# GpSimd's second addition for the dot products goes behind the stage's second gather; r follows it ahead of the third

## The reference

```
r = edge_vec / jnp.linalg.norm(edge_vec, axis=1, keepdims=True)
sh1 = SQRT3 * r
xs, xd = (x[edge_src], x[edge_dst])
v1 = jnp.concatenate([xs[:, 8:].reshape(E, 8, 3), xd[:, 8:].reshape(E, 8, 3)], axis=1)
vdot1 = jnp.einsum('euk,ek->eu', v1, sh1) / SQRT3
s_t = a1 * (jnp.einsum('eu,euw->ew', s1, Wss) + jnp.einsum('eu,euw->ew', vdot1, Wvv))
```

## Time and profile before

| | us |
|---|---|
| median of 3 runs | 6613.86 (6610.04 to 6614.21) |
| the profiled execution's own time | 6605.81 |
| its span | 6604.0 |
| PE busy | 5916.6 (90%) |
| DVE busy | 5987.5 (91%) |
| ACT busy | 4058.7 (61%) |
| POOL busy | 5021.9 (76%) |

### The profile page before, as it was taken

How to read it: one execution, slowest core, us unless ns; L and a number is a source line. 1 busy time by engine, 2 the same in 40 slices (tenths; PEclk the granted TensorE clock), 3 DMA queues, 4 the chain that set the end, 5 groups by cost and what they waited for, 6 DMA issues and landing times.

```text
span 6604.0 us, 217789 instructions
## 1 busy us (share of the span) xinstructions
PE 5916.6 (90%) x67802; PEld 5648.0 (86%) x67802; DVE 5987.5 (91%) x7727; ACT 4058.7 (61%) x12100; POOL 5021.9 (76%) x6871
## 2 busy tenths in 40 slices
PE   2999999999999999999999999999989999999997
PEld 2888888888888888888888888888888888888887
DVE  6999999999999999999999999999999999999998
ACT  3666666666666666666666666666666666666664
POOL 4777777777777777777777777777777777777774
PEclk9999999999999999999999999999999999999998
DMA  4444444444444444444444444444444444444442
GB/s 126 86 89 84 86 87 85 85 87 86 84 86 88 84 87 86 84 86 88 84 86 88 84 86 88 84 88 86 86 89 84 86 88 84 88 86 86 87 85 54
DMA packets 1671528, 569.93 MB, mean 86 GB/s; under 512 B 1535556, under 2 KB 1619493, under 8 KB 1670946
## 3 DMA queue, kind: packets, MB, share of 16 engines
q1 hardware_dynamic: 1568321, 516.43, 35.3%
q0 software_dynamic: 103168, 53.03, 6.0%
HBM read 302.19 MB, written 7.26 MB: 47 GB/s over the span
## 4 chain that ended last, share of the span: by engine, by line
PE 75%; issue 13%; DVE 5%; ACT 3%; another core or an unknown queue 3%; DVEq 1%; ACTq 0%; DMA 0%; POOL 0%; SPq 0%; POOLq 0%
PE p L982 42%; PE pw L977 18%; PE p L1068 4%; PE ph L965 2%; PE ph L954 2%; PE p L1061 2%; PE p L1063 1%; PE p L1029 1%; PE p L1011 1%; DVE prods L1275 1%; ACT hot_t L741 1%; PE p L1012 1%; DVEq L1434 1%; ACT osum L820 0%
## 5 line engine op out<-in xcount | busy, mean ns | idle before, releaser
L982 PE MATMUL p<-identity,prods 128*128 128x128 f32 x29016 | 3642.6, 279 | 7.8 <-issue 6.7
L647 POOL DMA_INDIRECT nodes<-x_rows,idx x3224 | 3114.5, 966 | 603.7 <-issue 515.9
L982 PEld LDWEIGHTS p<-identity,prods 128*128 128x128 f32 x29016 | 3292.0, 146 | 36.5 <-issue 12.3
L977 PE MATMUL pw<-w_stack,hid_t 128*128 128x128 bf16 x22568 | 1702.4, 223 | 116.2 <-issue 52.4
L977 PEld LDWEIGHTS pw<-w_stack,hid_t 128*128 128x128 bf16 x22568 | 1433.6, 100 | 216.7 <-issue 98.2
L1275 DVE TENSOR_TENSOR prods<-pw,M 128x1024 f32<-128x1024 f32 x806 | 977.1, 1212 | 38.5 <-PE pw L977 24.8
L1233 DVE TENSOR_TENSOR prods<-pw,V 128x2048 f32<-128x2048 f32 x403 | 914.4, 2269 | 9.4 <-ACT acc L926 6.3
L1252 DVE TENSOR_TENSOR prods<-pw,S 128x1024 f32<-128x1024 f32 x403 | 491.8, 1220 | 327.6 <-remote 190.7
L838 ACT ACTIVATE off_hot<-node_iota,off_base 128x42 f32<-128x42 f32 x3216 | 752.6, 317 | 13.0
L1285 DVE TENSOR_TENSOR prods<-pw,VT 128x1536 f32<-128x1536 f32 x403 | 705.2, 1750 | 23.9 <-PE pw L977 19.4
L594 POOL TENSOR_TENSOR msg<-th,late 128x128 f32<-128x128 f32 x403 | 164.0, 407 | 728.7 <-ACT th L819 390.8
(11 more groups left out here) (130 smaller groups left out, 8205.5 us busy)
## 6 DMA issues: line engine op xcount, KB each, us to landing
dstb<-in_dst SPq DMA_DIRECT2D x403, 504.0 KB
nodes<-x_rows,idx POOLq DMA_INDIRECT x3224
emb_stack<-emb_parts SPq DMA_DIRECT2D x2418, 20.0 KB
emb<-in_emb_t SPq DMA_DIRECT2D x403, 40.0 KB
hid_t<-hid_parts SPq DMA_TRANSPOSE x806
idx<-in_src SPq DMA_DIRECT2D x403, 4.0 KB
xw<-x SPq DMA_DIRECT2D x403, 7.9 KB
vecs<-in_vec SPq DMA_DIRECT2D x403, 12.0 KB
```

Source lines behind the costliest of these rows:

```text
L647: nc.gpsimd.indirect_dma_start(nodes[:, p, t, side, :], None, x_rows, bass.IndirectOffsetOnAxis(ap=idx[:, p, side, t:t + 1], axis=0)).then ...
L977: mm = nc.tensor.matmul(pw[:, slot, t, :], hid_t[:, layer, a.par, t, :], w2_stack[:, lo:lo + W], start=True, stop=True)
L982: return nc.tensor.matmul(out, column, identity[:, :], start=first, stop=last, is_transpose=True)
```

## The change

`along_rest` is cut in two. Its first addition (L614) stays between the first and the second gather. The second one, with its wait for `vr_two_done`, becomes `along_last` and is called behind the second gather, ahead of `directions`. So the program has r still between the second and the third gather, and the subtraction of the edge attributes alone between the third and the fourth.

```
             pool.wait_ge(vr_done, a.n(1, 1))
             nc.gpsimd.tensor_tensor(vr_two[:, :, :], vr[:, 0, :, :], vr[:, 1, :, :], ALU.add).then_inc(vr_two_done, 1)
+
+        def along_last(a):
+            p = a.par
             pool.wait_ge(vr_two_done, a.n(1, 1))
             nc.gpsimd.tensor_tensor(S[:, p, :, 2 * C:4 * C], vr_two[:, :, :], vr[:, 2, :, :], ALU.add
                                     ).then_inc(vdot_done, 1)
...
                     along_rest(two)
                 if zero is not None:
                     gathers(zero, 0, (1,))
+                if two is not None:
+                    along_last(two)
                 if one is not None and i != -1:
                     directions(one)
                 if zero is not None:
                     gathers(zero, 0, (2,))
```

## The result

The median of four runs went from 6614.03 us (6610.04 to 6622.14) to **6455.94 us** (6442.14 to 6466.6), a ratio of 0.9758 [0.9736, 0.9781]. The forecast was 6614 us with a range down to 6601, so 158 us were missed. The profiled execution of the changed kernel took 6466.6 us by its own time, 139 us less than that of before (6605.81).

A forecast was written before the change was run, and what follows sets the result against it. DVE (91%) and PE (90%) were taken to bound the kernel, POOL having slack ahead of L594. Terms summed to 0 in the turns and 0 at the start, so the 6613.86 us median gave 6614 us, range 6601 to 6628.

The forecast's parts named there:

- room for the later `S`: DVE's L1260 reads `S` at least 6.12 us after the addition; `S` 1.06 us later leaves 5.06 us, cost 0.
- the start gives nothing: In the first stage L1260 begins 1.06 us later, but another branch bounds the next step: cost 0.
- L1233 doesn't hold the addition: POOL's second addition runs unheld within DVE's product; the slower rival, a hold up to 2.27 us a turn, had 0.06.
- r stays at its time: On POOL, r and all that follows move by -0.07 to +0.01 us a turn, cost 0.
- the held gathers are still 28: Every fourteenth turn the second gather starts 1.32 us late; the addition behind it comes 2.23 us later, cost 0.
- L594's wait: POOL's wait for ACT, 728.7 us in 403 turns, at least 0.96 each, absorbs shifts ahead of it; stays near 728.
- that exchange: DVE and PE, nearly full, hand work to each other; DVE's largest idle, 327 us, is ahead of L1252.
- A gain of nothing: POOL's second gather begins 0.52 us sooner, but its rows are laid out a turn later, once all eight are there.
- The case for a gain of any kind: Faster rival: the wait between the two additions was on the path, so POOL's gain reaches it: 6586 us, chance 0.06.
- its one price, 28 us: Faster rival's size: 0.07 us a turn over 403 turns, from a gather hiding the gap between L614 and L616.

The follow-up runs named there:

- Both behind: Kernel before with both additions put behind the second gather, ahead of r: 6343.37 us, 0.9675 with late signals; 0.9996 and 0.9994 with signals on time.

## Why the prediction was wrong

**What held.** That L1260 has room for the later `S`: its only wait for the addition grew from 5.9 to 6.8 us (7.0 forecast). That the start gives nothing: 0.9996 in the run of the first turns alone. That L1233 doesn't hold the addition: 455 to 482 ns against 452 to 465 in the earlier trace rows, though 353 of the 403 additions now lie wholly inside that product, 250 before. The Trainium skill (SBUF — State Buffer, section "SBUF: two separate sides") has VectorE take the shared port in a two-port mode or with two operands in SBUF, and L1233 has one in PSUM: the trace agrees. That r stays at its time: it began some 0.04 us ahead of the addition's recorded end, where the bound was 0 to 0.08 behind; the size is nothing, but the lower bound was off. That the held gathers are still 28: they are, but the hold is smaller, an idle of 0.73 us in the median ahead of the second gather in place of 1.32. L594's wait went from 728.7 to 373.8 + 278.6 = 652.4 us and still takes up what POOL loses in nearly every turn.

**Which step failed.** Two sentences that together put the gain at nothing. "POOL is not part of that exchange unless one of its results comes late" took the waits for POOL's results to be the only way in which POOL can act. And of the second gather: "A gain of nothing, and its packets move by half a microsecond in a queue whose landings no engine is seen to wait for." What the runs show in their place: PE's signals are late in most turns on some chips, and where in the turn the lateness falls changes with the order of POOL's first slots, though its results are waited for no more than before (L1260 once, 6.8 us). If it falls on `osum_sum`, ACT stands for up to 2.7 us, then PE, and in part of those turns the low clock follows. In the changed kernel it falls more on `gates_sum` and the sums for `M`, and the run is 158 us shorter; that it lies beside other work there is read from the waits and was not tested by itself. How POOL's order reaches PE's signals stays open. The case for a gain of any kind had a chance of 0.06, and its one price, 28 us, was for another cause.

**What was in the rows.** The earlier trace rows had DVE's 190.7 us of remote waits, which the prediction called waiting for weights that PE has yet to fill, without looking at when those matmuls had ended; the turn at 1014 shows that they had. The greater row, 512.9 us for ACT's `osum_t`, was not weighed at all, and its releaser is named by neither an instruction nor a transfer. With such a row inside the exchange that bounds the kernel, a chance of 0.06 for a gain was too small, and a range of 13 us down was not made by the profile but by the argument about POOL alone. Over the kernels profiled where signals are late, that row stands at 305 to 513 us where the time stayed within 0.6% of before, and at 0 to 51 where it fell by 2.4% or more.

**Where the number held.** On the chips with signals on time the changed kernel is at 0.9988 and 0.9989 of before, within the 0.2% that was forecast, though the upper ends lie at 0.9999 and 1.0000: perhaps 0.1% for a reason that isn't known. The cover of L594 is thinner there than reckoned. The waits of the kernel of before on such a chip:

```profile
POOL msg L594 <- issue: 146.6, 184, 5.8
...
POOL msg L594 <- ACT th L824: 105.6, 173, 13.2
```

That is 252.2 us in 403 turns, 0.63 us in the mean in place of 1.81: two thirds of the slack ahead of L594 is there only where the signals are late. So the forecast of no change fits these two chips, but its cover had been read from a profile with late signals in it, which was luck.

## What stays open

What holds PE's signals on some chips was not found, and no run moved the lateness by itself: that it is what makes the change worth something rests on the two chips that have it and the two that don't. SP's small instructions are slow on the same chips: the register moves ahead of the load of `idx` have a mean of 174 ns in the profile of before (171 in that of the first turns alone) against 36 where signals are on time, so PE isn't the only one affected. SP's largest remote wait, 207.7 us at L441, is one for PE's `xd_mm` and shows only the same lateness again. Every execution timed here was also recorded with its span and granted clock; whether the signals are late when nothing is recorded isn't shown. Whether the earlier gather or the later `S` moves the lateness, and by which path, is open, as said above. And r ahead of the second gather costs some 0.6% on all three chips that ran it, late signals or not; POOL's idle ahead of gathers put down to "issue" grows there from 506.2 to 679.2 us with signals on time, but the cause was not tried. Both behind is the best version measured: 3.25% less than before where signals are late and even with it where they aren't.

## What to carry to other kernels

Before a reordering is costed at nothing, read every wait of the engines in the bounding exchange, also those that no instruction ends ("remote"): set the releasing work's end beside the waiter's start, and if there are microseconds between them, keep a case open in which any shift of neighbours moves them. A lowered clock beside a stall is a thing to test apart, by filling the stall: here that gave 0.5% of some 3%. And time a small change on a second chip: this one gave 2.4% on one, 2.7% on another (in the loop alone) and 0.1% on two others.

## What the runs showed of the hardware

The same kernel took 6614, 6552 and 6555 us on three chips and 6039 to 6046 us on two others, and the difference of 8 to 9% goes with PE's semaphore updates: for the sums of `osum_t` 2242 ns in the median on the first against 287 on those two. Two independent element-wise operations on POOL overlap by some 0.05 us in the records, dependent ones stand 0.08 apart, and two gathers in a row stand 0.31 apart where one behind an element-wise operation stands 0.16. One gather in 112 is held: its idle was 1.32 us behind both additions and 0.73 us with one of them moved behind it.
